# Sums of the exponentials beside the weighing, and a reordered start, in a one-core ViT block

## What is computed

```python
paths = sigmoid(x @ Wp + bp)                       # 8 heads of 5 values
agree = pq * pk + (1.0 - pq) * (1.0 - pk)
sim = cumprod(agree, axis=-1).sum(axis=-1) / DEPTH # causal mask, then softmax over keys
attn = softmax(sim, axis=-1)
ctx = attn @ (x @ Wv)
h = layernorm(h + ctx @ Wo)
```

## Time and profile before

| | |
|---|---|
| median of 3 runs | 158.72 us (158.41 to 159.54) |
| profiled execution | 160.36 us, its span 158.6 us |
| TensorE matmul busy | 150.6 us, 95% of the span |
| VectorE busy | 82.7 us, 52% |
| ScalarE busy | 61.8 us, 39% |
| GpSimd busy | 48.7 us, 31% |

### The profile page before, as it was taken

The page is one execution under the profiler, slowest core; times in us unless marked ns, Lnnn a source line. Parts: engine busy times, 40 slices in busy tenths (PEclk is TensorE's granted clock), DMA queues, the critical chain, the costliest instruction groups (busy, mean ns, idle before and its releaser), DMA issues.

```text
span 158.6 us, 2922 instructions
## 1 busy us (share of the span) xinstructions
PE 150.6 (95%) x1118; PEld 118.1 (74%) x1118; DVE 82.7 (52%) x160; ACT 61.8 (39%) x133; POOL 48.7 (31%) x125
## 2 busy tenths in 40 slices
PE   6999989999999899999999999999999999999980
PEld 5777677776677588677887876887888878878860
DVE  2422346756679790777705777912968215730042
ACT  0411212535052555637458344656607442044200
POOL 5040001030335540547404533611743105540011
PEclk9999999999999999999999999999999999999998
DMA  4999999910000000000000010000001000101000
GB/s 150 275 247 266 246 319 399 390 48 4 0 0 0 10 0 0 4 0 8 4 33 0 0 37 0 0 33 4 0 0 37 33 0 0 35 4 35 0 33 33
DMA packets 5614, 10.67 MB, mean 67 GB/s; under 512 B 747, under 2 KB 4416, under 8 KB 5344
## 3 DMA queue, kind: packets, MB, share of 16 engines
q1 hardware_dynamic: 5146, 10.07, 21.0%
q10 hardware_dynamic: 454, 0.40, 0.9%
HBM read 9.26 MB, written 1.21 MB: 66 GB/s over the span
## 4 chain that ended last, share of the span: by engine, by line
PE 82%; DVE 7%; DMA 3%; POOL 3%; issue 2%; SPq 0%; ACT 0%; POOLq 0%
PE bank_s L566 20%; PE bank_z L598 18%; PE bank_z L460 6%; PE bank_p L475 3%; DMA x_rows<-in_x 3%; PE bank_s L434 3%; PE bank_s L503 3%; PE bank_p L449 3%; PE bank_w L519 3%; PE bank_p L476 3%; PE bank_o L537 2%; PE bank_w L598 2%; PE bank_o L538 2%; PE bank_w L523 2%; PE bank_o L449 2%; PE bank_z L449 2%
## 5 line engine op out<-in xcount | busy, mean ns | idle before, releaser
L566 PE MATMUL bank_s<-hnT,w 128*128 128x256 f32 (+1 forms) x160 | 32.9, 364 | 0.0
L566 PEld LDWEIGHTS bank_s<-hnT,w 128*128 128x128 f32 x160 | 28.7, 190 | 3.8 <-ACT hnT L750 0.4
L598 PE MATMUL bank_z<-w,act 128*128 128x256 f32 x128 | 30.0, 381 | 0.0
L598 PEld LDWEIGHTS bank_z<-w,act 128*128 128x128 f32 x128 | 23.5, 190 | 3.1 <-issue 0.2
L740 ACT ACTIVATE act<-bank_s,vec_cols 128x256 f32<-128x256 f32 (+1 forms) x40 | 16.1, 455 | 19.5 <-PE bank_s L566 19.5
L348 POOL TENSOR_TENSOR rstd<-var,exponents 128x3 f32<-128x3 f32 (+1 forms) x10 | 8.7, 872 | 37.1 <-DVE var L868 37.0
L855 DVE RECIPROCAL recip<-bank_w 128x222 f32<-128x222 f32 (+1 forms) x11 | 16.4, 1494 | 1.0 <-PE bank_w L523 1.0
L862 DVE BATCH_NORM_STATS2 stats<-bank_o 128x6 f32<-128x256 f32 (+1 forms) x10 | 4.3, 430 | 19.0 <-PE bank_o L538 18.9
L722 ACT ACTIVATE phi_q<-bank_p 128x222 f32<-128x222 f32 (+1 forms) x11 | 3.9, 352 | 24.8 <-PE bank_p L485 24.8
L460 PE MATMUL bank_z<-xT,wT 128*128 128x288 f32 x48 | 12.9, 414 | 0.0
L337 POOL TENSOR_TENSOR signs<-signs 111x8 f32<-111x8 f32 (+1 forms) x11 | 4.3, 389 | 27.1 <-ACT signs L707 27.1
(11 more groups left out here) (114 smaller groups left out, 232.6 us busy)
## 6 DMA issues: line engine op xcount, KB each, us to landing
x_rows<-in_x SPq DMA_DIRECT2D x5, 576.0 KB, 10.8
q<-in_L_ffn_fc_q SPq DMA_DIRECT2D x2, 1024.0 KB, 18.6
s<-in_L_ffn_fc_scales SPq DMA_DIRECT2D x2, 1024.0 KB, 21.0
out<-fin SPq DMA_DIRECT2D x9, 128.0 KB, 1.7
x_rows<-in_x SPq DMA_DIRECT2D x2, 288.0 KB, 4.7
w_rows<-in_L_tok_W SPq DMA_DIRECT2D x2, 256.0 KB, 6.5
w_rows<-in_L_tok_W ACTq DMA_DIRECT2D x1, 256.0 KB, 3.0
wvp<-in_L_attn_Wv SPq DMA_DIRECT2D x1, 256.0 KB, 8.3
```

The costliest lines, as they stand in the source:

```text
L566: last = mm(block[:, i], w1[:, e, f * 128:(f + 1) * 128], hnT[p % 2][:, e, 0:n], start=(e == 0), stop=(e == E2 - 1))
L598: last = mm(z_bank(b)[0:w, 0:D], act2[:, f, in_pair(b)], w2[:, f, :], start=(f == 0), stop=(f == FB - 1))
```

## The change

It does five things.

1. `weigh`: the sums of the exponentials are no longer four products of 222 columns behind both groups of heads, but four of 111 columns behind each group.
2. Start: `turn_weight(1)` and `turn_block(1)` are put between the products of block 0, `turn_weight(2)` and `turn_block(2)` ahead of the second half of those of block 1, and `turn_vectors` behind them. DVE's `x_columns(2)` goes ahead of `position_columns`.
3. The waits follow: `turn_vectors` waits for three copies by DVE, and the wait for the position values moves from `turn_block(2)` to `turn_block(3)`.
4. `keep_busy` issues 4 and 5 transposes in place of 2 and 3 before the two halves of block 0.
5. For a = 3, `turn_normed(1)` moves from ahead of the six products of `project(3, 1)` to a place behind the first two of them.

```diff
-    KEEP_BUSY = {"before the weights": 10, "before the first half": 2, "before the second half": 3}
+    KEEP_BUSY = {"before the weights": 10, "before the first half": 4, "before the second half": 5}
...
-                pe.wait_ge(xT_dve, 2)
+                pe.wait_ge(xT_dve, C)
...
-                    if n == 2 and ih == 0:
+                    if n == C and ih == 0:
                         pe.wait_ge(posb_step, 1 + E2)
...
-            def project(c, e, turn=None):
+            def project(c, e, turn=None, turn_at=KT):
                 for k in range(KT):
-                    if turn is not None and k == KT - 2:
+                    if k == turn_at:
                         turn_normed(turn)
...
-                sums = by_group(bank_w[:, HG * R:2 * HG * R], n)
-                for i in range(HQ):
-                    last = mm(sums[32 * i:32 * (i + 1)], ones_keys[0:n, :], probs[0:n, i, :, 0:n], start=True, stop=True)
+                    for i in range(HQ):
+                        last = mm(bank_w[32 * i:32 * (i + 1), (HG + g) * R:(HG + g) * R + n], ones_keys[0:n, :],
+                                  probs[0:n, i, g, 0:n], start=True, stop=True)
...
             project_channel(0, 0)
-            project_channel(0, 1)
             turn_weight(1)
+            project_channel(0, 1, outputs=(0,))
             turn_block(1)
+            project_channel(0, 1, outputs=(1,))
             project_channel(1, 0)
+            turn_weight(2)
+            turn_block(2)
+            project_channel(1, 1)
             turn_vectors()
-            turn_weight(2)
-            project_channel(1, 1)
-            turn_block(2)
             project_channel(2, 0)
             turn_block(C)
...
-                if a in TURN_AT and a != 2:
+                if a in TURN_AT and a > 3:
                     turn_normed(TURN_AT[a])
...
-                    project(3, 0, turn=TURN_AT[a])
+                    project(3, 0, turn=TURN_AT[a], turn_at=KT - 2)
...
-                    project(3, 1)
+                    project(3, 1, turn=TURN_AT[a], turn_at=2)
...
             by_patch(2)
+            x_columns(2)
             position_columns()
-            x_columns(2)
             class_tokens()
```

## The result

The changed kernel takes 157.23 us in the median of 6 executions (156.46 to 157.56), against 158.89 us (158.41 to 160.35) for the kernel before beside it. The ratio is 0.9876, with a 95% interval of 0.9829 to 0.9923. So it is 1.2% faster; the forecast was 157.0 us. Executions over 1.5% above the fastest of their kernel are left out of every ratio here. The profiled execution takes 157.19 us with a span of 155.5 us. Before these were 160.36 and 158.6: the two profiles lie 3.1 us apart, the medians 1.7.

The account below looks back on a forecast made before the run. TensorE, busy 95% of the span, was taken as the bound. Start -1.07, weighing +0.17 and turn -0.82 sum to -1.72: profiled 160.36 becomes 158.6, and 1.64 less for the median gives 157.0 us (range 155.7 to 158.2).

Parts of the forecast that it names:

- Term 1: Block 0: more keep-busy transposes make the first products start slightly later, +0.04 us (0 to +0.13).
- The base: Starting point of the sum: the profiled execution, 160.36 us, with the median taken 1.64 us below the profiled one.
- Rival A: Start: added transposes raise TensorE's clock at about 7.6 us, not 11; about 1.15 us more gained, 155.85; chance 0.2.
- A's sign: Profile after, block 0: `bank_p`'s first four passes take less than 2 us, which would show Rival A.
- Terms 2 to 4: Start's order: block 1's waits go, -0.98; block 2, -0.23; DVE's copies for blocks 3 and 4 late, +0.10 us.
- term 3: Block 2: losses of 0.67 go but the weight turn's 0.44 wait comes, -0.23 us (-0.67 to +0.2).
- Term 5: Weighing: sums cut into more rounds cost 0.015 us a tile, 11 times, +0.17 us (0 to +0.33).
- Rival D: Weighing: the added rounds show their weight loads, 2.35 us on top, 159.35, slower than before; chance 0.04.
- Term 6: Turn for a = 3: two products first remove the wait for DVE's block, -0.82 us (-0.4 to -0.85).
- Rival C: Turn for a = 3 still waits as DVE's block comes later; half the gain goes, 157.4; chance 0.08.

Follow-up runs that it names:

- the one profile above: DVE's `by_patch(3)` put ahead of `position_columns`, against the changed kernel with 222-column sums and block 2's weights turned earlier: 156.66 us, ratio 0.9856; profiled execution 157.92 us.

## Why the prediction was right, and where it wasn't

The direction, the size and the largest terms held. By its own steps:

**Term 1, the keep-busy** (+0.04): the step that failed. It was costed as work added, with an earlier clock as a rival of 0.2. What the runs show is that it changes the share of long executions, and in the profiled ones the moment of the clock's rise: ten of 57 executions of the kernel before were over 1.0 us above their median, three of six with 2 and 3 in the new order had the longer span, none of 12 with 4 and 5 in the kernel before; without any, the change gains nothing. In the kernel before the share is small, so the step is worth little there: +0.03 us by the medians, -0.35 by the ratio, with an interval that includes zero. That the medians give what the term said is luck, since its reason was wrong; in the new order 2 and 3 in place of 4 and 5 cost 0.47 us (157.85 against 157.38), where the term has a gain of 0.04. How many of the long executions are the clock's and how many come from late patches, as in the one profile above, stays open.

**The base.** I reckoned the sum from the profiled execution and took over its distance to the median, 1.64 us. That was sound for terms 2 to 6, which don't hang on the clock. The sum's own result, 158.6 for the profiled execution, was off: it took 157.19, next to its median of 157.23. Most of the 1.64 came from the late clock of the profile before and was gone in the profile after; since it was only carried over, the forecast of the median didn't suffer. Rival A's 155.85 was wrong: it took 1.15 off a median in which, by their spans, most executions already had the early clock. A's sign was seen (first products under 2 us), its time was not: the right reading was that the profile before was late, as its 160.36 against 158.41 to 159.54 hinted.

**Terms 2 to 4, the start's order** (-1.11 together): 17.54 to 16.52 between two profiles with the clock up early, -1.02. Block 1's gaps went whole, block 2's wait for `wT` came as told, and DVE's `x_pat` of block 4 is what TensorE waits for. Set against the kernel before with the same keep-busy and an early clock, the parts are -0.97 for block 1 (forecast -0.98), -0.14 for block 2 (-0.23) and +0.09 for what DVE makes late (+0.10). So term 3 was mis-sized: its 0.67 had in it that the first products of block 2 would need 0.97, and behind the narrow tiles of `turn_vectors` `bank_p` still takes 1.07 (20.13 to 21.20).

**Term 5, the sums** (+0.17): right in sign, three times too large. A weighing costs 0.006 more and not 0.015, 0.06 in all. The mis-sized part is the round of 111 columns, which the sum took at 0.097 and which starts 0.095 behind the last in the sums of the profile after; the round of 222 takes 0.187 as reckoned. The term's lower bound was 0, so the range held it.

**Rival D** fell: the switch from sums back to values costs no more than the other, 34.44 - 34.25 = 0.19. The Trainium skill's rule (TensorE: Matmul & The Clock Gate, Part 3: Packing small matmuls), by which weight loads in the same rows aren't hidden, would have cost 2.35 us; the two added rounds of each tile cost 0.006.

**Term 6, the turn** (-0.82):

```profile
57.68 0.57 PE L566 MATMUL bank_s<-hnT,w 128*128 128x160 f32 x3
```

57.68 - 53.61 = 4.07 us from the signs to the first hidden product before, 54.49 - 51.24 = 3.25 after, -0.82. Alone it gave -0.83. Where DVE's block comes at the earlier of its two moments, as in the profile with the start's order alone, the wait that goes is 0.55 and the term about -0.67. Rival C fell: the margin was 52.33 - 52.06 = 0.27, forecast 0.2.

Together -1.02 + 0.06 - 0.82 = -1.78. With the keep-busy that is -1.75 by the medians and -2.1 by the ratios. Measured is -1.7 by the medians, and by the ratio 1.2% of 158.89, that is -2.0 us (-1.2 to -2.7). The two profiles' 3.1 us are 1.02 + 0.82 - 0.06, the clock's 1.00 behind the first products, and 0.37 by which these start earlier (8.12 and 8.49), a part that falls to the clock's rise and to when the first patches land; which of the two had how much I didn't separate.

## What to carry to other kernels

In a kernel whose bounding engine has no long waits left, put the timeline's stretches against the same instructions run back to back: 0.1 to 0.6 us were lost at each place where a transpose, its copy and its reader followed each other directly, and other work between them got nearly all of it back. A step that only fills idle time before the dense part is not to be costed as work added alone; ask whether it moves the clock's rise in a share of the executions, look at single executions and not at the median alone, and check in a profile whether a long one is the clock's or a late transfer's. Of a copy on another engine's list, first ask what stands just ahead of it there: moving it up past something earlier does nothing.

## What the runs showed of the hardware

TensorE's clock rose where the engine had done nothing but transposes. In the profile with the start's order alone the row before the first products reads:

```profile
6.75 0.71 PE L434 MATMUL bank_s<-ident,x_pat 96*128 96x96 f32 x6
```

That is full speed 0.8 us before the first product at 7.51, and the same stands in the profile after, at 7.36. It also fell again before the first product, after 1.26 us without work, in the run with 2 and 3; after 1.79 us without work, in the run with `by_patch(3)` ahead, it didn't.

A weighing's rounds in 32-wide column tiles can be cut at no cost worth naming: 888 columns in six rounds or in eight took 0.896 and 0.902 us, with twice as many weight loads of about 0.11 us for the sums.
